# One more round of attention ahead of the expert stage, with the routing work spread differently over VectorE's queue

## The reference

```python
q = (x @ Wq + bq).reshape(b, s, h, d)      # likewise k, v; x is xn here
qr, qi = (q * c, q * sn)                   # c, sn: cos and sin of phase
scores = (einsum('bshd,bsgd->bshg', qr, kr) + einsum('bshd,bsgd->bshg', qi, ki)) * scale
out = einsum('bshg,bsgd->bshd', softmax(scores), v)
s = swapaxes(out, 1, 2).reshape(b, s, h * d) @ Wo + bo
gates = sinkhorn((xn @ router_w.T + router_b) / temp)   # 3 iterations
topk_vals, topk_idx = top_k(gates, 2)
f = xn + sum(gate_k * (relu(xn @ wg[e]) * (xn @ wp[e])) @ wo[e])
x = x + s * silu(f)
```

## Time and profile before

| | |
|---|---|
| median of three runs | 1590.97 us (1590.71 to 1592.67) |
| the profiled execution | 1590.1 us, span of its instructions 1588.3 us |
| mean granted TensorE clock | 0.988 of full speed |
| busy: TensorE, VectorE, ScalarE, GpSimd | 1530.9, 972.8, 728.8, 793.0 us |

### The profile page before, as it was taken

The page is one execution under the profiler, slowest core; times in us unless marked ns, Lnnn a source line. Parts: engine busy times, 40 slices in busy tenths (PEclk is TensorE's granted clock), DMA queues, the critical chain, the costliest instruction groups (busy, mean ns, idle before and its releaser), DMA issues.

```text
span 1588.3 us, 32794 instructions
## 1 busy us (share of the span) xinstructions
PE 1530.9 (96%) x11408; PEld 1166.3 (73%) x11408; DVE 972.8 (61%) x1880; ACT 728.8 (46%) x1205; POOL 793.0 (50%) x945
## 2 busy tenths in 40 slices
PE   5999699989999999999999999999999999999997
PEld 2546566668888888888888888776666776666773
DVE  7567989953333333333333333577889788888777
ACT  4766334413333333333333333546456565555552
POOL 4637589813433444433444333253574564853456
PEclk9999899989999999999999999999999999999999
DMA  9989852265233231323211231255555666455464
GB/s 327 396 314 324 301 187 78 76 217 189 68 124 108 82 126 64 97 95 111 77 54 57 71 146 51 90 167 166 172 187 189 205 200 207 156 168 172 155 206 147
DMA packets 175351, 251.23 MB, mean 158 GB/s; under 512 B 15336, under 2 KB 122656, under 8 KB 175072
## 3 DMA queue, kind: packets, MB, share of 16 engines
q1 hardware_dynamic: 160576, 211.48, 39.1%
q0 software_dynamic: 12960, 35.41, 6.8%
q10 hardware_dynamic: 1664, 2.26, 0.4%
HBM read 149.58 MB, written 99.50 MB: 157 GB/s over the span
## 4 chain that ended last, share of the span: by engine, by line
PE 89%; DVE 6%; DMA 2%; ACT 1%; issue 1%; SPq 1%; ACTq 0%; DVEq 0%
PE ps L1145 23%; PE ps L1080 21%; PE ps L1091 13%; PE ps L1164 12%; PE ps L1027 6%; PE ps L1154 4%; PE ps L1048 2%; PE ps L1127 2%; PE ps L996 2%; PE ps L924 1%; DMA WR<-w_d 1%; PE ps L980 1%; PE ps L914 1%; DVE UN L1230 1%; SPq L502 1%
## 5 line engine op out<-in xcount | busy, mean ns | idle before, releaser
L1145 PE MATMUL ps<-WR,FR 128*128 x1620 | 407.9, 401 | 1.9 <-DMA WR<-w_d 1.8
L1145 PEld LDWEIGHTS ps<-WR,FR 128*128 128x128 f32 x1620 | 296.2, 189 | 60.2 <-issue 3.0
L649 POOL DMA_INDIRECT y_d<-AUX x135 | 133.3, 987 | 351.6 <-ACT AUX L868 351.6
L1656 DVE TENSOR_TENSOR AUX<-AUX,ps 128x512 f32<-128x512 f32 x135 | 92.9, 688 | 342.0 <-ACT AUX L856 342.0
L817 ACT ACTIVATE WM<-ps,bcs,trig 128x512 f32<-128x512 f32 x256 | 252.2, 1016 | 85.9 <-PE ps L1080 78.9
L1596 DVE TENSOR_SCALAR WM<-ps,vec,trig 128x512 f32<-128x512 f32 x256 | 243.6, 993 | 61.2 <-ACT WM L817 60.5
L1091 PE MATMUL ps<-WM,XTJ 128*128 128x512 f32 x512 | 237.1, 600 | 0.0
L856 ACT ACTIVATE AUX<-ps 128x512 f32<-128x512 f32 x135 | 80.9, 599 | 318.5 <-PE ps L1145 318.5
L1080 PE MATMUL ps<-XH,WH 128*128 128x512 f32 x512 | 204.8, 400 | 6.1 <-issue 3.8
L1164 PE MATMUL ps<-WR,ABR 128*128 x1080 | 209.4, 292 | 0.0
L1080 PE MATMUL ps<-XH,WL 128*128 128x512 f32 x512 | 199.7, 390 | 0.0
(11 more groups left out here) (238 smaller groups left out, 2199.1 us busy)
## 6 DMA issues: line engine op xcount, KB each, us to landing
US<-u_d SPq DMA_DIRECT2D x63, 512.0 KB, 5.4
u_d<-UN SPq DMA_DIRECT2D x120, 256.0 KB, 2.0
WR<-w_d SPq DMA_DIRECT2D x96, 256.0 KB, 6.0
AUX<-y_d SPq DMA_DIRECT2D x32, 512.0 KB, 5.6
WM<-in_L_attn_x_dram SPq DMA_DIRECT2D x16, 512.0 KB, 9.5
xn_d<-WM SPq DMA_DIRECT2D x32, 256.0 KB, 7.3
w_d<-USR SPq DMA_DIRECT2D x16, 512.0 KB, 4.9
AUX<-xn_d SPq DMA_DIRECT2D x16, 512.0 KB, 6.1
```

Of the source, the lines that this page charges most:

```text
L649: e.indirect_dma_start(y_d, bass.IndirectOffsetOnAxis(toks[:, m - 5:m - 4], 0), YS[:, (m - 5) % 2, :], None).then_inc(s_y[(m - 5) % 2], 16)
L1145: mm = e.matmul(b[:, :], x, WR[:, bass.ds(off[m] + (2048 * z + 1024 * a + 512 * k), 512)], start=(k == 0 and x is xh and z == 0), stop=(k ...
L1656: e.tensor_tensor(HS[:, m % 2, :], GR[:, :], mP[m % 2][:, :], ALU.mult).then_inc(s_h, 1)
```

## The change

`QE` becomes 5: five rounds run ahead of the experts and eleven after them. The rounds whose rows are stored and finished later remain four (`QF = QE - 1` takes QE's place there): round 4's sums are mixed in round 5 and finished at once, and the `host` rounds become 6, 8, 10, 12. The `side` functions move: `top2` from chunk 21 of round 0 to chunk 0 of round 1 (so behind round 0's softmax), `ranks` to chunk 9, `slotted` to chunks 15 and 17, `sink_end` on TensorE to chunk 6. `place` begins at chunk 22 of round 1, at another pace, and ends at chunk 15 of round 4. `listed` runs behind chunk 17, `weigh` behind chunk 20 and its copy (`permuted`) behind chunk 22 of round 4. The first weighted sum waits for `ranks` (`s_rk`) rather than for both `slotted`. GpSimd makes `XTJ` for rounds 2, 3 and 4 between its one-hots (after tiles 5, 29 and 54). Two semaphores are split, and two small copies are added that carry one.

```diff
-QE = 4
+QE = 5
+QF = QE - 1
-            if (q, c) >= (1, 20):
-                pace += 1.5 if c < 16 else 2.4 if c < 24 else 4.0
+            if (q, c) >= (1, 22):
+                pace += 1.6 if c < 16 else 2.6 if c < 24 else 0.5
-        host = {QE + 1 + 2 * k: k for k in range(QE)}
+        host = {QE + 1 + 2 * k: k for k in range(QF)}
...
-                    if QE < q < NQ - 1:
+                    if QE <= q < NQ - 1:
                         store_c(q - 1)
                         load_c(q)
...
-            load_c(QE)
+            load_c(QF)
             segment(QE, NQ)
...
                 if n == 20:
-                    xtj(2)
...
-                elif n == 54:
-                    xtj(3)
+                elif n in (5, 29, 54):
+                    xtj((5, 29, 54).index(n) + 2)
...
-            side[24 + 1] = sink_end
+            side[24 + 6] = sink_end
...
                 if n == 0:
-                    e.wait_ge(s_disp, 1)
+                    e.wait_ge(s_rk, 1)
...
+            side[24 * (QE - 1) + 20] = weigh
...
             gt(0)
-            weigh()
...
+                e.tensor_copy(off, off).then_inc(s_rk, 1)
...
-            side[21] = top2
-            side[24 + 3] = ranks
-            side[24 + 6] = lambda: slotted(0, oh1)
-            side[24 + 9] = lambda: slotted(1, oh2)
+            side[24] = top2
+            side[24 + 9] = ranks
+            side[24 + 15] = lambda: slotted(0, oh1)
+            side[24 + 17] = lambda: slotted(1, oh2)
             side[48 + 23] = experts
+            side[24 * (QE - 1) + 17] = listed
+            side[24 * (QE - 1) + 22] = permuted
...
-                    if q == QE - 1:
-                        listed()
...
             xgl(0)
-            e.wait_ge(s_gp, 1)
-            e.tensor_copy(GP[:, :, :, :].rearrange("p i k q -> p (i k q)"), pD[:, 0:128]).then_inc(s_gp, 1)
```

More of the change, by code:

```diff
@@ L207, in program @@
         s_disp, s_eoff = sem("s_disp"), sem("s_eoff")
-        s_dum, s_oa, s_ob, s_od, s_sel, s_gp = (sem(n) for n in ("s_dum", "s_oa", "s_ob", "s_od", "s_sel", "s_gp"))
+        s_dum, s_oa, s_ob, s_oc, s_od, s_sel, s_gp, s_rk = (
+            sem(n) for n in ("s_dum", "s_oa", "s_ob", "s_oc", "s_od", "s_sel", "s_gp", "s_rk"))
         s_wl, s_wlo, s_xgl = sem("s_wl"), sem("s_wlo"), sem("s_xgl")
@@ L246, in program @@
                     firsts.setdefault(slots[k - 3], []).append(j // 4)
-        host = {QE + 1 + 2 * k: k for k in range(QE)}
+        assert sum(len(lists[s]) for s in slots if s < (QE - 1, 16)) == 2 * NT
+        host = {QE + 1 + 2 * k: k for k in range(QF)}
         def ro(n):
-            return RO[:, n % 2, :] if n < 4 * QE - 4 else RO4[:, n % 4, :]
+            return RO[:, n % 2, :] if n < 4 * QF else RO4[:, n % 4, :]
         def raw(i):
@@ L540, in _ @@
                 store_last(n)
-            e.wait_ge(s_o, 64 * (NQ - QE))
-            e.wait_ge(s_es, 64 * QE)
+            e.wait_ge(s_o, 64 * (NQ - QF))
+            e.wait_ge(s_es, 64 * QF)
         @block.gpsimd
@@ L828, in segment @@
                             side[24 * q + c]()
-                        if q > QE and c == 18:
+                        if q >= QE and c == 18:
                             silu(q - 1)
@@ L1452, in experts, with listed, permuted @@
                 e.tensor_scalar(eoff[:, 0:NM], iom[:, :], -6144.0, 16384.0, ALU.mult, ALU.add).then_inc(s_eoff, 1)
+            def listed():
+                e.wait_ge(s_od, 2 * NT)
+                e.wait_ge(s_dum, 1)
+                none, ids = cum[:, 0:NM], cum[:, 136:136 + NM]
+                wi, hi, lo = (AUX[:, 2048 + NW * i:2048 + NW * i + NM].bitcast(I32) for i in range(3))
+                e.tensor_scalar(none, pD[:, 0:NM], 0.0, None, ALU.is_equal)
+                ch(e.tensor_scalar(wi, pD[:, 0:NM].bitcast(I32), 16, None, ALU.arith_shift_right))
+                e.tensor_tensor(none, none, dum, ALU.mult)
+                e.tensor_scalar(hi, wi, 0x7C, 7, ALU.bitwise_and, ALU.logical_shift_left)
+                ch(e.tensor_scalar(lo, wi, 3, None, ALU.bitwise_and))
+                e.tensor_scalar(wi, wi, 7, 2, ALU.arith_shift_right, ALU.logical_shift_left)
+                ch(e.tensor_tensor(ids, hi, lo, ALU.add))
+                ch(e.scalar_tensor_tensor(none, ids, -256.0, none, ALU.add, ALU.add))
+                ch(e.tensor_tensor(ids, none, wi, ALU.add))
+                ch(e.tensor_copy(toks, ids))
+                e.tensor_scalar(gidx, toks, N - 1, None, ALU.bitwise_and).then_inc(s_gi, 1)
+                for h in range(H):
+                    ins = e.tensor_tensor(seli[:, h, :, :].rearrange("p i (r a) -> p (i r) a", a=H),
+                                          ident[:, :, None].broadcast_to([128, 128, H]),
+                                          eh[:, h, None, :].broadcast_to([128, 128, H]), ALU.mult)
+                ins.then_inc(s_sel, 1)
+            def permuted():
+                e.wait_ge(s_gp, 1)
+                e.tensor_copy(GP[:, :, :, :].rearrange("p i k q -> p (i k q)"), pD[:, 0:128]).then_inc(s_gp, 1)
             side[18] = gates
             side[19] = top1
-            side[21] = top2
-            side[24 + 3] = ranks
-            side[24 + 6] = lambda: slotted(0, oh1)
-            side[24 + 9] = lambda: slotted(1, oh2)
+            side[24] = top2
+            side[24 + 9] = ranks
+            side[24 + 15] = lambda: slotted(0, oh1)
+            side[24 + 17] = lambda: slotted(1, oh2)
             side[48 + 23] = experts
+            side[24 * (QE - 1) + 17] = listed
+            side[24 * (QE - 1) + 22] = permuted
             def xt(q, k):
```

76 lines of the change are left out of this document (27 added, 49 removed).

## The result

The changed kernel took 1600.47 us (median of 9 runs, 1594.08 to 1607.21), the kernel before beside it 1590.97 (9 runs, 1588.19 to 1595.3): a ratio of 1.005, 95% interval [1.0031, 1.0068], so slower by 8.0 us by the ratio. The forecast of +6.3 us, 1597.3, holds in sign and size. Its terms don't all hold, and that is what the experiments are for.

What follows compares the result with a forecast made beforehand. VectorE was taken to bound round 0's scores to round 1's end, the weight DMAs the passage into the experts. 2.8 + 1.1 + 3.7 - 0.8 - 0.5 = 6.3 us on 1590.97 gave 1597.3, range 1588 to 1602.5.

Steps and rivals of the forecast that it cites:

- Round 0's scores to round 2: Stretch through round 1: round 2 starts at 231.6 against 230.2; net of placements 2.8 us worse.
- The stall: TensorE's 10.8 us wait moves six chunks later in round 1: 1.4 us ahead of chunk 5, 9.5 ahead of chunk 6.
- softmax 11.75: VectorE's softmax of round 0 takes 11.75 us, as in the profile of the kernel before.
- rival S: Rounds 0 and 1: VectorE loses less to GpSimd blocking, chunk 6 starts 4 us earlier; +2.3 us, 1593.3; chance 0.14.
- Placements, 1.4 + 1.1: Before round 2, placements cost 0.5 us instead of 1.9; later, more between projections, fewer at scores: 1.1 us worse.
- weigh, 3.7: Round 4, behind chunk 20: weigh's products stand where TensorE has no gap, 3.7 us worse.
- the credit of 0.5: Round 2's scores: small waits may go with fewer column one-hots on VectorE, at most 0.5 us gained.
- rival G: Three rounds: GpSimd's one-hots, held by XTJ stops or slotted(1), delay placements some 2 us each; 1603; chance 0.06.
- The passage: Round 4 into the experts: weight DMAs end it, so nothing is saved; 0.8 us credit for gathers no longer beside them.
- W: Passage after round 4: weights aren't last to arrive, giving -1.8 us, 1589.2, or under 1587.8 with shorter DMA; chance 0.06.
- The moved round: Round moved ahead of the experts costs TensorE the same, 47.03 us; round 5's load wait 0, up to 3.
- Rival F: Round 1: later stall doesn't come if VectorE idles over 6 us between 180 and 230; -5.5 us, 1585.5; chance 0.10.

Runs made afterwards that it cites:

- the four traces of the changed kernel: The changed kernel's first measurement, its unedited repeat and two repeats whose added TensorE register loads never reached the chip: ratios 1.005, 1.0085, 1.0045 and 1.006.
- the first trace: Profiled execution of the changed kernel's first measurement, without a further edit: 1600.47 us, ratio 1.005, span 1594.0 us.
- The second trace: The changed kernel measured again without an edit: 1603.71 us, ratio 1.0085, span 1598.6 us.
- the one with the order alone: The kernel before with only VectorE's order changed (top2, ranks, slotted later, TensorE's sink_end behind chunk 6), experts still after round 3: ratio 1.0023.
- the trace without it: The changed kernel with listed, weigh and permuted put back behind the scores of the last round before the experts: ratio 1.0074.
- the last trace: The changed kernel with 5 register loads added on TensorE ahead of the first up product, which never reached the chip: ratio 1.006.

## Why the prediction was right, and where its steps were off

To compare steps I take the four traces of the changed kernel (spans 1594.0, 1598.6, 1603.3, 1609.2; mean 1601.3) and the one of before (1588.3). The difference of 13.0 is more than the ratios show (1.006 in the mean, 9.5 us), as traces are single executions. It splits thus, in us, taking the mean of the four: start of round 0's scores -0.5; from there to round 2 -0.3; round 2 to the last weighted sum, less one round of 47.03, +9.3; passage -0.1; experts up to round 6 -0.5; the later rounds' excess +4.9; tail +0.1.

That 5.7 us in the first trace (1594.0 against 1588.3) stand so near the forecast's 6.3 is luck. In that trace one term came out 4.2 us better than forecast, the stretch before round 2, and two 4.9 us worse, round 2 to the last sum and the later rounds. By the ratios of four measurements the change costs 7.2 to 13.5 us, in the mean 9.5, and the forecast is 3 us short.

- Round 0's scores to round 2: forecast 231.6 against 230.2, +1.4 gross; measured -0.3 in the mean (-2.8, -1.0, +0.7, +2.1). The stall was where I put it, at 7.6 to 8.1 us, and the 1.4 ahead of chunk 5 was gone: 10.9 forecast, 8.08 in the first trace. What failed is the term "softmax 11.75" as a constant: it was 8.94 in the first trace, since the small subtractions took 255 ns, and that difference of 2.8 is the whole of the stall's. In the other three it was 9.1 to 9.4. This is rival S by mechanism, to a smaller size. In these three instruction stops in the scores of rounds 0 and 1, which the forecast hadn't, took 2.1 to 3.1 us of it back. The second trace has the subtractions at 448 ns, the one with the order alone at 644. The Trainium skill, "SBUF — State Buffer", section "Who interferes with whom", says that a VectorE instruction with two SBUF inputs contends with a GpSimd one that reads SBUF, by an exclusive lock; the traces agree in that the long subtractions end 0.03 us after an instruction of GpSimd, which was busy in all of them (7.7 us of 10 beside the 255 ns). Such a term needs both ends in the sum, not one value.
- Placements, 1.4 + 1.1, and weigh, 3.7, with 0.5 off: 5.7 forecast for round 2 to the last sum, 9.3 measured (7.3 in the first trace). Weigh is right, 3.68 in the trace, 3.5 by the trace without it. What was missing is the half clock behind weigh (1.7 us in three of the four traces) and behind the stop at the end of round 1's scores (about 1 us in two), 1.8 in the mean. The other 1.8 are in the rows too. The wait ahead of round 2's last scores didn't go, as the credit of 0.5 had it; it grew by 1.0 (1.66 to 1.93 in the four traces against 0.65), under `XTJ` moved beside `experts`. In all traces of kernels with that step moved the wait is 1.65 us or more, in all without it 0.81 or less; no run moved the step alone. That XTJ stop was weighed for the one-hots alone (rival G), not for what GpSimd does to VectorE. The rest is small: the scores of round 3, which now lie in the way of a next round, take 8.3 us with two placements, where those of round 5 take 7.6.
- The passage: forecast -0.8; -0.9 in the first trace, -0.1 in the mean of four. "What is saved is nothing" held. The wait before the tile was ended by the weights in all four traces, 8.55 to 10.2 us. Rivals W and G didn't occur.
- The moved round: 47.03 on either side was right, but not all that moves with it. `host` counts from `QE + 1`, so one more round ahead of the experts turned the host rounds from odd to even. The later rounds' excess grew by 3.2 us in the first trace and 4.9 in the mean: 2.3 of that is stops for instructions in the scores, 1.5 waits for VectorE ahead of the weighted sums, and the rest mostly half clock behind them. This term was missing from the sum altogether. The experiments put 2 to 5 us to the parity of the host rounds, with scatter. The load wait in round 5 (0 to 3) was 0.
- Rival F, the hidden stall, didn't occur, but the point from which I let it decide was ill put: VectorE was idle for over 6 us between 180 and 230 (3.4 by 188, 3.1 from 218), as I had asked, and the stall stood all the same, as it comes ahead of that idle time. What matters is slack before chunk 6, and there is none.

## What to carry to other kernels

Where two chains of nearly one length end at one instruction, as the lists and the weights here, work moved out of one of them is paid where it lands and gains nothing until the other is shortened too; look for the second chain before pricing the first. A stall on a ring's slowest reader moves with that reader's work and doesn't go away. And when a stage is shifted, look at everything numbered relative to it: here the parity of the host rounds was worth 2 to 5 us, as much as a term of the sum, and a GpSimd step moved beside VectorE's work 1 us. A wait that the profile names issue may be one for another engine: see what ended just before it.

## What the runs showed of the hardware that was not expected

- TensorE stops, without a wait in the program, at places that are a multiple of 256 of its instructions apart, for 0.3 to 2.8 us, and goes on 1.1 to 1.6 us after the DMA of a 16 KB block of instructions has landed. Scores are where it shows; 512 instructions pass there in 7.9 us.
- What VectorE pays beside GpSimd is decided by where the two meet: the same subtraction took 175 to 1282 ns, a cast of 8 columns 0.17 and 1.13 us, and the long ones ended with an instruction of GpSimd.
- After a stop of some 2 us the clock can be at half: behind 2.81 us in the last trace, the stage 1356 to 1359 has 0.50, and round 11 took 48.3 us. Behind 32 small products in 3.68 us (weigh) the same was seen in five traces of eight, though TensorE never stood; why in some and not in others is open.
- Runs of one kernel spread over 13 us, and mostly with the mean granted clock: over the nine runs of the changed kernel the correlation is -0.81 (span 1592.3 us at 0.991, 1605.5 at 0.985). Between the kernels it doesn't differ (0.9876 against 0.9877 before), so it isn't what made the change slower. The span of a single trace stood up to 8 us from the mean of four; a term read from one is worth reading in a second.
